# Cross attention: softmax sums from pairs of key tiles, experts moved by four to five steps, small products ahead of value and sum products in a step

## The chip, the cores and the metric

One Trainium2 chip, one of its cores. The metric is the device time of one execution of the whole program in microseconds, taken as the median of several runs.

## The reference

A decoder of two layers with a layer norm after each of six sublayers, on 8 batches of 256 tokens of width 512. The change touches the last but one sublayer, cross attention with the context, whose heads and positions are read crosswise (the 256 tokens are the channels, 512 features the positions), and the order of the last one, experts chosen by a router, beside it:

```python
qh = q.reshape(B, h, dq, Lq)          # B = 8 batches, h = 8 heads, dq = 32, Lq = 512
kh = k.reshape(B, h, dq, Lk)          # k = v = the context, Lk = 512
scale = 1.0 / jnp.sqrt(jnp.asarray(dq, dtype=q.dtype))
qk = jnp.einsum('bhdq,bhdl->bhql', qh, kh) * scale
sm = jax.nn.softmax(qk, axis=-1)
ret = jnp.einsum('bhql,bhdl->bhdq', sm, vh)
return gamma * ret
...
x = _layernorm(x + _L1_xattn_ref(x, ctx_2048, ctx_2048, L1_xattn_gamma), axis=-1)
x = _layernorm(x + _L1_ffn_ref(x, ...), axis=-1)   # top 2 of 8 experts of rank 16
```

## The kernel before, in words

All sublayers run one after the other in one program. The function of the change, `l1_cross_and_experts` (line 1799), does the last two together. Each engine has a queue of its own, written out by hand: all five walk the same list `steps()` (line 1882), 16 steps `g` per batch `b`, and at each step an engine does what its `if` lines name. Engines meet only at semaphores, so an engine's queue order is fixed and a wait in it holds all behind it.

A batch is two halves `t` of four heads (32 rows each, 128 partitions). A half has four key tiles `k` of 128 keys; a tile is four units (one per head), done in two steps of two units each. In a step TensorE makes, 11 steps ahead (`LEAD`), rough scores of two heads for 128 queries (`rough_scores`, L2358), from rounded operands; VectorE takes their maxima (`maxima`, L2212), which TensorE turns (`turn_largest`, L2366), ScalarE rounds (`round_largest`, L2129), and SyncE puts as a 97th row behind the stacked operands (`place_largest`, L1975). This is why the scores are made twice: the second time (`scores`, L2376) they come out transposed, keys on the partitions, with the maximum subtracted. The 96 other rows are high and low parts of x and context, copied together by `stack` (L1956): 24 copies of 128 KB per batch from SyncE's queue, for which `take_lo` (L1937, on GpSimd for batches 1 to 7) makes the low parts.

ScalarE takes the exponential of each unit (`exps`, L2135) into one of 12 buffers `pT`. Once per key tile TensorE multiplies four units with the values (`values`, L2388, into `v_ps`) and four units with a matrix of ones (L2391, into `d_ps`), which adds up the softmax's denominators over all four tiles. At the end of a half ScalarE reads both out (`read_out`, L2142 and L2145). The denominators take a detour: SyncE lays one row per head over partitions (`lay_sums`, L1985), VectorE inverts them (`invert`, L2221), SyncE writes them to memory (`keep_inverses`, L1991) and reads them back spread over the partitions (`spread_inverses`, L1999). GpSimd multiplies and adds the residual (`residual`, L2055 and L2061). The last half is inverted directly (L2218).

Then follow, for the batch before, the norm (`statistics` L2226, `power` L2067 to L2073, `apply` L2151) and the experts: `turn_x` (L2401), `turned` (L2157), `project` (L2412), `shift`, `exponential`, `gate`, `choose`, `picks`, `weigh` on VectorE and ScalarE, `turn_hidden` (L2420), `hidden` (L2171), `out` (L2429, L2430), `add_experts` (L2295), a second norm and `store` (L1966). Two banks `a_ps` serve rough scores and all of these products in turn, in the order of the steps (`slot_uses`); a product waits until the use before last of the banks has been read. The score products have two banks `s_ps`, one per unit: a unit waits for the exponential two units before.

## Time and profile before

| what | us |
|---|---|
| median of 3 runs | 2101.18 (2098.77 to 2101.21) |
| the profiled execution's own time | 2102.42 |
| its span, first to last instruction | 2100.3 |
| TensorE (PE) busy | 1864.2 (89%) |
| VectorE (DVE) busy | 1145.9 (55%) |
| ScalarE (ACT) busy | 851.1 (41%) |
| GpSimd (POOL) busy | 331.6 (16%) |

Busy time is the union of an engine's instructions over all sublayers. The granted clock is the share of TensorE's full clock of 2.4 GHz; at 0.5 it runs at 1.2 GHz. In the rows, L and a number is a line of the kernel, `out<-in` are the tiles it writes and reads, "x8" the records merged into one line, and in brackets stands how long the engine was idle before and which instruction or transfer ended that. SPq is the queue of transfers that SyncE issues; one product of two float32 operands is two records, so four products of values are "x8". TensorE's durations overlap each other, so its pace is read from start to start.

### The profile page before, as it was taken

The page shows a single profiled execution, that of the slowest core. Times are in us where ns is not written, and L with a number is a line of the kernel's source. Part 1 is how long each engine was busy: PE and PEld are TensorE (multiplying, and loading weights), DVE is VectorE, ACT ScalarE, POOL GpSimd, SP SyncE. Part 2 cuts the span into 40 slices and gives each one's busy share as a digit, 9 for nine tenths or more (in the row PEclk, how much of TensorE's full clock was granted, in tenths as well). Part 3 has the DMA queues.
Part 4 walks back from the last instruction along what each step waited for, and adds up shares of the span by engine and source line. Part 5 has one row for each costly group of instructions (what it writes and reads, how often), then busy time and mean ns, then how long its engine had stood idle before and what let it go on. Part 6 is the DMA issues. An engine that isn't in the chain of part 4 may idle for free. (4 is left out here: it accounts for less than half of the span.)

```text
span 2100.3 us, 30928 instructions
## 1 busy us (share of the span) xinstructions
PE 1864.2 (89%) x11568; PEld 1425.5 (68%) x11568; DVE 1145.9 (55%) x2133; ACT 851.1 (41%) x2040; POOL 331.6 (16%) x414
## 2 busy tenths in 40 slices
PE   6979999999976799999999987899996498899994
PEld 5869998998964688888888876677774133333332
DVE  3446444444435565555555436788876535555543
ACT  2225333333323343333333214666674145555552
POOL 0000000000011112111111001333332212223211
PEclk9989999999988899999999998999998589999997
DMA  3122000000012221111110013000101644444400
GB/s 103 44 97 71 21 21 21 21 21 21 26 54 78 83 79 46 36 31 41 46 36 16 11 41 120 11 32 32 51 21 61 174 115 102 112 115 124 102 22 25
DMA packets 83664, 119.83 MB, mean 57 GB/s; under 512 B 15221, under 2 KB 31221, under 8 KB 83517
## 3 DMA queue, kind: packets, MB, share of 16 engines
q1 hardware_dynamic: 83516, 117.86, 19.5%
q8 instruction: 93, 1.52, 0.3%
q14 instruction: 55, 0.44, 0.1%
HBM read 75.42 MB, written 16.98 MB: 44 GB/s over the span
## 5 line engine op out<-in xcount | busy, mean ns | idle before, releaser
L2212 DVE TENSOR_REDUCE e_nbx<-e_a_ps 128x2 f32<-128x1024 f32 x128 | 153.2, 1214 | 103.0 <-PE e_a_ps L2358 102.9
L1164 PE MATMUL yp<-ccy,toep 128*128 128x288 f32 x640 | 181.8, 435 | 19.7 <-POOL ccy L892 13.6
L2135 ACT ACTIVATE e_pT<-e_s_ps 128x512 f32<-128x512 f32 x256 | 139.0, 597 | 126.7 <-PE e_s_ps L2376 123.8
L1442 ACT ACTIVATE p<-p,nb,rq 128x128 f32<-128x128 f32 (+1 forms) x256 | 136.9, 541 | 94.8 <-DVE nb L1539 94.8
L1164 PEld LDWEIGHTS yp<-ccy,toep 128*128 128x128 f32 x640 | 126.0, 205 | 55.7 <-POOL ccy L892 14.8
L80 PE MATMUL q_ps<-a_xt_hi,wq_hi 128*128 128x256 f32 x512 | 151.7, 296 | 4.2 <-DVE wo_lo L112 4.1
L82 PE MATMUL q_ps<-a_xt_hi,wq_lo 128*128 128x256 f32 x512 | 146.5, 286 | 0.0
L81 PE MATMUL q_ps<-a_xt_lo,wq_hi 128*128 128x256 f32 x512 | 146.3, 286 | 0.0
L1062 DVE SCALAR_TENSOR_TENSOR hm<-gu_ps,us_col,sg 128x256 f32<-128x256 f32 x88 | 42.3, 480 | 184.1 <-ACT sg L971 184.1
L514 ACT ACTIVATE ex<-ex 128x512 f32<-128x512 f32 x64 | 40.4, 632 | 213.8 <-DVE ex L567 213.8
L1399 POOL TENSOR_TENSOR p<-p,rs 128x512 f32<-128x512 f32 x64 | 94.2, 1472 | 195.5 <-DVE rs L1546 195.5
L2376 PE MATMUL e_s_ps<-qs,ks 97*128 97x512 f32 x256 | 108.5, 485 | 18.4 <-DMA qs<-e_xh 14.2
L971 ACT ACTIVATE sg<-gu_ps,gs_col 128x256 f32<-128x256 f32 x88 | 41.6, 473 | 189.8 <-PE gu_ps L82 189.7
L545 DVE TENSOR_TENSOR tl<-t_ps,th 128x512 fp32r<-128x512 f32 x64 | 44.3, 692 | 132.7 <-ACT th L506 132.7
L80 PE MATMUL o_ps<-wo_hi,th 128*128 128x512 f32 x256 | 106.7, 417 | 1.9 <-DVE tl L545 1.9
L80 PE MATMUL gu_ps<-m_xt_hi,wg_hi 128*128 128x256 f32 x352 | 100.3, 285 | 8.2 <-DVE m_xt_lo L1054 8.2
L231 POOL TENSOR_TENSOR n_rstd<-n_mv,eps 128x2 f32<-128x2 f32 x16 | 3.1, 197 | 634.2 <-DVE n_mv L225 634.2
L80 PEld LDWEIGHTS q_ps<-a_xt_hi,wq_hi 128*128 128x128 f32 x512 | 99.9, 195 | 4.7 <-issue 4.5
L81 PE MATMUL o_ps<-wo_lo,th 128*128 128x512 f32 x256 | 101.2, 395 | 0.0
L82 PE MATMUL o_ps<-wo_hi,tl 128*128 128x512 f32 x256 | 101.1, 395 | 0.0
L80 PE MATMUL gu_ps<-m_xt_hi,wu_hi 128*128 128x256 f32 x352 | 100.1, 284 | 0.0
L81 PEld LDWEIGHTS q_ps<-a_xt_lo,wq_hi 128*128 128x128 f32 x512 | 99.8, 195 | 0.0
(296 smaller groups left out, 4904.7 us busy)
## 6 DMA issues: line engine op xcount, KB each, us to landing
x_after<-n_r SPq DMA_DIRECT2D x16, 512.0 KB, 2.8
toep<-padded_kernels SPq DMA_DIRECT2D x32, 256.0 KB, 3.6
qs<-e_xh SPq DMA_DIRECT2D x64, 128.0 KB, 2.5
ks<-e_ch SPq DMA_DIRECT2D x64, 128.0 KB, 2.5
x<-in_x SPq DMA_DIRECT2D x8, 512.0 KB, 4.3
a_x<-in_x SPq DMA_DIRECT2D x8, 512.0 KB, 4.5
ring<-in_wqT SPq DMA_DIRECT2D x8, 512.0 KB, 4.6
ring<-in_woT SPq DMA_DIRECT2D x8, 512.0 KB, 3.8
```

The source lines that it names most:

```text
L80: pe.matmul(out, whi, xhi, start=start, stop=False)
L81: pe.matmul(out, whi, xlo, start=False, stop=False)
L82: return pe.matmul(out, wlo, xhi, start=False, stop=stop)
L545: dve.tensor_tensor(tl[:], t_ps[:], th[:], ALU.subtract).then_inc(tl_done, 1)
L971: act.activation(sg[:], gu_ps[n % 2][:, 0, :], ACT.Silu, scale=gs_col[:, j:j + 1]).then_inc(sg_done, 1)
L1062: dve.scalar_tensor_tensor(hm[:], gu_ps[n % 2][:, 1, :], us_col[:, j:j + 1], sg[:], ALU.mult, ALU.mult).then_inc(hm_done, 1)
L1164: last = pe.matmul(yp[:, lo % 2, 0:NCOL], toep[h % 2][:, (lo - li) * P:(lo - li + 1) * P], ccy[h % 2][:, li, 0:NCOL], start=(li == 0), sto ...
L1399: pool.tensor_tensor(tile, tile, r, ALU.mult).then_inc(pn_done, 1)
L1442: act.activation(p[n % 3][:, h, part[t]], p[n % 3][:, h, part[t]], ACT.Exp, bias=nb[i][:, t, h:h + 1], scale=rq[u][:, t:t + 1], accum_out= ...
L2135: act.activation(pT[u % NPT][:], s_ps[u % 2][:], ACT.Exp).then_inc(e_done, 1)
L2212: dve.tensor_reduce(heads, slot("pair", n)[:], AX.X, ALU.max, negate=True).then_inc(nb_done, 1)
L2376: pe.matmul(s_ps[u % 2][:], ks[b % 2][0:KX, t, j, k * P:(k + 1) * P], qs[b % 2][0:KX, t, j, :], start=True, stop=True).then_inc(s_mm, 1)
```

## The change

Sums: instead of adding up four key tiles by four blocks of products with ones, GpSimd adds the exponentials of tiles 0 and 1 (`add_early`), VectorE those of tiles 2 and 3 (`add_late`), and TensorE makes two blocks of products per half (`sum_up`). The buffers of exponentials are 13 instead of 12; `nbr`, `dsb`, `vsb` and `rec` have one buffer instead of two. `scores` makes two units after one wait for both exponentials of the pair before. The values come one step later, and in a step they and the sums stand behind the small products. The experts of a batch, both norms, `read_out`, the inverses and `residual` come one to five steps later, and the list is five steps longer. At the start `stack(0)` stands ahead of `load(1)` and gamma, the weights come after `place_largest(0)`, and the two memsets of the operands' row of ones come later.

The diff, cut to its core (waits on renamed semaphores and the one-buffer indices are left out in part):

```diff
-NPT = 12
+NPT = 13
...
-        nbr = [sb(f"e_nbr{i}", [P, D], F32R) for i in range(2)]
+        nbr = sb("e_nbr", [P, D], F32R)
...
-        dsb = [sb(f"e_dsb{i}", [P, D]) for i in range(2)]
-        vsb = [sb(f"e_vsb{i}", [P, D]) for i in range(2)]
+        early = [sb(f"e_early{j}", [P, D]) for j in range(HT)]
+        late = [sb(f"e_late{j}", [P, D]) for j in range(HT)]
+        dsb, vsb = sb("e_dsb", [P, D]), sb("e_vsb", [P, D])
...
-        rec = [sb(f"e_rec{i}", [P, D]) for i in range(2)]
+        rec = sb("e_rec", [P, D])
...
+    stack(0)
     load(1)
     sp.dma_start(gcol[:], gamma.partition_broadcast(P)).then_inc(g_loaded, 16)
-    stack(0)
-    next_load(2)
-    residual(0)
...
     for b, step, g in steps():
+        if g == -1:
+            next_load(2)
+            residual(0)
...
         if step == 0 and 0 < b + 1 < B:
             stack(b + 1)
-        if step in (2, 10) and 0 <= 2 * b - 1 + step // 8 < LAST:
+        if step in (4, 12) and 0 <= 2 * b - 1 + step // 8 < LAST:
             lay_sums(2 * b - 1 + step // 8)
-        if step in (4, 12) and 0 <= 2 * b - 1 + step // 8 < LAST:
-            keep_inverses(2 * b - 1 + step // 8)
-        if step in (5, 13) and 0 <= 2 * b - 1 + step // 8 < LAST:
-            spread_inverses(2 * b - 1 + step // 8)
         if step in (6, 14) and 0 <= 2 * b + 1 + step // 8 < 2 * B:
             place_largest(2 * b + 1 + step // 8)
-        if step == 6 and 0 <= b - 2 < B:
+        if step in (6, 14) and 0 <= 2 * b - 1 + step // 8 < LAST:
+            keep_inverses(2 * b - 1 + step // 8)
+        if step in (7, 15) and 0 <= 2 * b - 1 + step // 8 < LAST:
+            spread_inverses(2 * b - 1 + step // 8)
+        if step == 9 and 0 < b + 1 < B:
+            residual(b + 1)
+        if step == 10 and 0 <= b and b + 3 < B:
+            next_load(b + 3)
+        if step == 11 and 0 <= b - 2 < B:
             store(b - 2)
-        if step == 8 and 0 < b + 1 < B:
-            residual(b + 1)
-        if step == 8 and 0 <= b and b + 3 < B:
-            next_load(b + 3)
     sp.wait_ge(stored, 16 * B)
...
+    def add_early(n, j):
+        u = UNITS // 2 * n + j
+        pool.wait_ge(e_done, u + HT + 1)
+        if n:
+            pool.wait_ge(d_mm, 2 * n - 1)
+        pool.tensor_tensor(early[j][:], pT[u % NPT][:], pT[(u + HT) % NPT][:], ALU.add).then_inc(early_done, 1)
...
-        if step == 4 and 0 <= b - 2 < B:
-            power(b - 2, mv6, mv6_done, y6_done, rstd6, ve6_done, rstd6_done, nm6, nm6_done)
-        if step == 6 and 0 <= b - 1 < B:
+        if step in (4, 5, 12, 13) and 0 <= b < B:
+            add_early(2 * b + step // 8, step % 2 * 2)
+            add_early(2 * b + step // 8, step % 2 * 2 + 1)
+        if step == 0 and 0 <= b - 1 < B:
+            residual(b - 1, 0)
+        if step == 8 and 0 <= b - 1 < B:
             residual(b - 1, 1)
         if step == 6 and b + 2 < B:
             scale_x(b + 2)
-        if step == 8 and 0 <= b - 1 < B:
+        if step == 9 and 0 <= b - 2 < B:
+            power(b - 2, mv6, mv6_done, y6_done, rstd6, ve6_done, rstd6_done, nm6, nm6_done)
+        if step == 10 and 0 <= b - 1 < B:
             power(b - 1, mv5, mv5_done, y5_done, rstd5, ve5_done, rstd5_done, nm5, nm5_done)
         if step == 10 and b + 2 < B:
             take_lo(pool, b + 2, "cl")
-        if step == 12 and b + 2 < B:
+        if step == 14 and b + 2 < B:
             take_lo(pool, b + 2, "xl")
-        if step == 14 and 0 <= b < B:
-            residual(b, 0)
...
     def exps(u):
         act.wait_ge(s_mm, u + 1)
         if u >= NPT:
+            n, k = divmod((u - NPT) // HT, NQ)
             act.wait_ge(pv_mm, (u - NPT) // HT + 1)
+            if k < 2:
+                act.wait_ge(early_done, HT * n + (u - NPT) % HT + 1)
+            else:
+                act.wait_ge(late_done, HT * n + (u - NPT) % HT + 1)
         act.activation(pT[u % NPT][:], s_ps[u % 2][:], ACT.Exp).then_inc(e_done, 1)
     def read_out(n):
         act.wait_ge(pv_mm, NQ * (n + 1))
-        if n >= 2:
-            act.wait_ge(laid[n % 2], 16 * HT * (n // 2))
-        act.activation(dsb[n % 2][:], d_ps[:], ACT.Copy).then_inc(o_read, 1)
-        if n >= 2:
-            act.wait_ge(added5, n - 1)
-        act.activation(vsb[n % 2][:], v_ps[:], ACT.Copy, scale=gcol[:]).then_inc(o_read, 1)
+        if n:
+            act.wait_ge(added5, n)
+        act.activation(vsb[:], v_ps[:], ACT.Copy, scale=gcol[:]).then_inc(v_read, 1)
+        act.wait_ge(d_mm, 2 * n + 2)
+        if n:
+            act.wait_ge(laid[(n - 1) % 2], 16 * HT * ((n - 1) // 2 + 1))
+        act.activation(dsb[:], d_ps[:], ACT.Copy).then_inc(d_read, 1)
...
     act.wait_ge(g_loaded, 16)
     for b, step, g in steps():
-        if step == 1 and 0 <= b - 2 < B:
+        if step == 5 and 0 <= b - 2 < B:
             hidden(b - 2)
-        if step == 11 and 0 <= b - 1 < B:
+        if step == 15 and 0 <= b - 1 < B:
             turned(b - 1)
         if 0 <= g < PAIRS_IN_ALL:
             exps(2 * g)
             exps(2 * g + 1)
-        if step in (2, 10) and 0 <= 2 * b - 1 + step // 8 < 2 * B:
+        if step == 1 and 0 <= b - 2 < B:
+            exponential(b - 2)
+        if step in (3, 11) and 0 <= 2 * b - 1 + step // 8 < 2 * B:
             read_out(2 * b - 1 + step // 8)
-        if step == 5 and 0 <= b - 2 < B:
-            apply(b - 2, nm6, nm6_done, rstd6, y6_done)
         if step in (5, 13) and 0 <= 2 * b + 1 + step // 8 < 2 * B:
             round_largest(2 * b + 1 + step // 8)
-        if step == 7 and 0 < b + 1 < B:
+        if step == 9 and 0 < b + 1 < B:
             context(b + 1)
         if step == 8 and b + 2 < B:
             round_hi(b + 2, "ch")
-        if step == 9 and 0 <= b - 1 < B:
+        if step == 10 and 0 <= b - 2 < B:
+            apply(b - 2, nm6, nm6_done, rstd6, y6_done)
+        if step == 12 and b + 2 < B:
+            round_hi(b + 2, "xh")
+        if step == 12 and 0 <= b - 1 < B:
             apply(b - 1, nm5, nm5_done, rstd5, y5_done)
-        if step == 10 and b + 2 < B:
-            round_hi(b + 2, "xh")
-        if step == 13 and 0 <= b - 1 < B:
-            exponential(b - 1)
 @block.vector
...
+    def add_late(n, j):
+        u = UNITS // 2 * n + 2 * HT + j
+        dve.wait_ge(e_done, u + HT + 1)
+        if n:
+            dve.wait_ge(d_mm, 2 * n)
+        dve.tensor_tensor(late[j][:], pT[u % NPT][:], pT[(u + HT) % NPT][:], ALU.add).then_inc(late_done, 1)
...
         dve.tensor_tensor(rr[b % 2][:], slot("out", b)[:], rr[b % 2][:], ALU.add).then_inc(added6, 1)
-    for u in range(2):
+    def one_row(u):
         dve.memset(ks[u][KX - 1:KX, :, :, :].bitcast(F32), 1.0).then_inc(set_up, 1)
     take_lo(dve, 0, "cl")
     take_lo(dve, 0, "xl")
-    dve.wait_ge(set_up, 5)
-    dve.wait_ge(g_loaded, 16)
+    dve.wait_ge(set_up, 3)
     for b, step, g in steps():
-        if step == 3 and 0 <= b - 2 < B:
+        if step == 1 and 0 <= b - 2 < B:
+            shift(b - 2)
+        if step == 8 and 0 <= b - 2 < B:
             add_experts(b - 2)
-        if step == 13 and 0 <= b - 1 < B:
-            shift(b - 1)
         if 0 <= g + LEAD < PAIRS_IN_ALL:
             maxima(g + LEAD)
+        if g == -3:
+            one_row(0)
         if b == 0 and step == 0:
+            one_row(1)
             dve.wait_ge(w_loaded, 64)
             dve.tensor_scalar(bias[:, 0, 0:E], bias[:, 0, 0:E], BONUS, None, ALU.add).then_inc(prepared, 1)
             dve.wait_ge(prepared, 3)
+        if step in (7, 15) and 0 <= b < B:
+            add_late(2 * b + step // 8, 0)
+            add_late(2 * b + step // 8, 1)
+        if step in (0, 8) and 0 <= 2 * b - 1 + step // 8 < 2 * B:
+            add_late(2 * b - 1 + step // 8, 2)
+            add_late(2 * b - 1 + step // 8, 3)
+        if step == 2 and 0 <= b - 2 < B:
+            gate(b - 2)
+            choose(b - 2)
         if step == 3 and 0 <= b - 2 < B:
+            picks(b - 2)
+            weigh(b - 2)
+        if step in (6, 14) and 0 <= 2 * b - 1 + step // 8 < 2 * B:
+            invert(2 * b - 1 + step // 8)
+        if step == 8 and 0 <= b - 2 < B:
             statistics(b - 2, added6, b - 1, st6, st6_done, mv6, mv6_done)
-        if step in (3, 11) and 0 <= 2 * b - 1 + step // 8 < 2 * B:
-            invert(2 * b - 1 + step // 8)
-        if step == 8 and 0 <= b - 1 < B:
+        if step == 10 and 0 <= b - 1 < B:
             statistics(b - 1, added5, T * b, st5, st5_done, mv5, mv5_done)
-        if step == 14 and 0 <= b - 1 < B:
-            gate(b - 1)
-            choose(b - 1)
-        if step == 15 and 0 <= b - 1 < B:
-            picks(b - 1)
-            weigh(b - 1)
...
-    def scores(u):
-        b, t, k, j = unit(u)
-        if k == 0:
-            pe.wait_ge(stacked[j], 16 * 6 * (b + 1))
-            pe.wait_ge(biased, 16 * HT * (T * b + t + 1))
-        if u >= 2:
-            pe.wait_ge(e_done, u - 1)
-        pe.matmul(s_ps[u % 2][:], ks[b % 2][0:KX, t, j, k * P:(k + 1) * P], qs[b % 2][0:KX, t, j, :],
-                  start=True, stop=True).then_inc(s_mm, 1)
+    def scores(g):
+        for u in (2 * g, 2 * g + 1):
+            b, t, k, j = unit(u)
+            if k == 0:
+                pe.wait_ge(stacked[j], 16 * 6 * (b + 1))
+                pe.wait_ge(biased, 16 * HT * (T * b + t + 1))
+        if g:
+            pe.wait_ge(e_done, 2 * g)
+        for u in (2 * g, 2 * g + 1):
+            b, t, k, j = unit(u)
+            pe.matmul(s_ps[u % 2][:], ks[b % 2][0:KX, t, j, k * P:(k + 1) * P], qs[b % 2][0:KX, t, j, :],
+                      start=True, stop=True).then_inc(s_mm, 1)
     def values(n):
...
         b, t, k, _ = unit(HT * n)
         pe.wait_ge(e_done, HT * (n + 1))
...
             pe.wait_ge(vt_done, b + 1)
         for j in range(HT):
             e = t * P + j * CX
-            pe.matmul(v_ps[j * CX:(j + 1) * CX, :], vt[b % 2][:, k, e:e + CX], pT[(HT * n + j) % NPT][:],
-                      start=(k == 0), stop=(k == NQ - 1), skip_group_check=True, tile_position=(0, j * CX))
+            last = pe.matmul(v_ps[j * CX:(j + 1) * CX, :], vt[b % 2][:, k, e:e + CX],
+                             pT[(HT * n + j) % NPT][:], start=(k == 0), stop=(k == NQ - 1),
+                             skip_group_check=True, tile_position=(0, j * CX))
+        last.then_inc(pv_mm, 1)
+    def sum_up(n, parts, done, first):
+        pe.wait_ge(done, HT * (n + 1))
+        if first and n:
+            pe.wait_ge(d_read, n)
         for j in range(HT):
-            last = pe.matmul(d_ps[j * CX:(j + 1) * CX, :], ones[:], pT[(HT * n + j) % NPT][:],
-                             start=(k == 0), stop=(k == NQ - 1), skip_group_check=True,
-                             tile_position=(0, j * CX))
-        last.then_inc(pv_mm, 1)
+            last = pe.matmul(d_ps[j * CX:(j + 1) * CX, :], ones[:], parts[j][:], start=first, stop=not first,
+                             skip_group_check=True, tile_position=(0, j * CX))
+        last.then_inc(d_mm, 1)
     def turn_x(b):
         pe.wait_ge(y5_done, T * b + T)
         if 0 <= g + LEAD < PAIRS_IN_ALL:
             rough_scores(g + LEAD)
         if 0 <= g < PAIRS_IN_ALL:
-            scores(2 * g)
-            scores(2 * g + 1)
+            scores(g)
         if g == 1:
             pe.wait_ge(set_up, 5)
-        if g % 2 and 0 <= (g - 3) // 2 < T * NQ * B:
-            values((g - 3) // 2)
         if step == 0 and 0 <= b - 2 < B:
+            project(b - 2)
+        if step == 4 and 0 <= b - 2 < B:
             turn_hidden(b - 2)
-        if step == 2 and 0 <= b - 2 < B:
-            out(b - 2)
         if step in (5, 13) and 0 <= 2 * b + 1 + step // 8 < 2 * B:
             turn_largest(2 * b + 1 + step // 8)
-        if step == 7 and 0 < b + 1 < B:
+        if step == 7 and 0 <= b - 2 < B:
+            out(b - 2)
+        if step == 9 and 0 < b + 1 < B:
             turn_context(b + 1)
-        if step == 10 and 0 <= b - 1 < B:
+        if step == 14 and 0 <= b - 1 < B:
             turn_x(b - 1)
-        if step == 12 and 0 <= b - 1 < B:
-            project(b - 1)
+        if g % 2 == 0 and 0 <= (g - 4) // 2 < T * NQ * B:
+            values((g - 4) // 2)
+        if step in (0, 8) and 0 <= 2 * b - 1 + step // 8 < 2 * B:
+            sum_up(2 * b - 1 + step // 8, early, early_done, True)
+        if step in (2, 10) and 0 <= 2 * b - 1 + step // 8 < 2 * B:
+            sum_up(2 * b - 1 + step // 8, late, late_done, False)
```

## Rows read from the trace of the kernel before

**Rows 1.** Stretches: length, busy PE, PEld, DVE, ACT, POOL, clock, DMA share, GB/s

```profile
1716.00:2052.00 336.00, 306.47 (x1658) 123.54 (x1658) 173.85 (x320) 187.00 (x333) 81.90 (x94) 0.94 0.39 100
1961.00:2009.00 48.00, 45.27 (x252) 18.21 (x254) 27.37 (x53) 26.59 (x49) 7.89 (x13) 0.96 0.41 101
```

**Rows 2.** Timeline, two steps of the loop in batch 1 (start, duration, both us)

```profile
1716.26 0.50 PE L2358 MATMUL e_a_ps<-e_ch,e_xh 32*128 32x512 f32 x2
...
1716.69 0.73 PE L2376 MATMUL e_s_ps<-qs,ks 97*128 97x512 f32 x2
...
1717.23 1.09 ACT L2135 ACTIVATE e_pT<-e_s_ps 128x512 f32<-128x512 f32 x2 [2.10 <-PE e_s_ps L2376]
...
1718.86 1.07 PE L2388 MATMUL e_v_ps<-e_pT,e_vt 128*32 128x512 f32 x8
...
1719.74 1.04 PE L2391 MATMUL e_d_ps<-e_pT,e_ones 128*32 128x512 f32 x8
...
1720.71 0.50 PE L2358 MATMUL e_a_ps<-e_ch,e_xh 32*128 32x512 f32 x2
```

**Rows 3.** Timeline, the turn of a batch on SyncE, VectorE and GpSimd

```profile
1715.17 0.67 SPq L1956 DMA_DIRECT2D qs<-e_xh  x1
...
1731.10 2.78 SPq L1985 DMA_DIRECT2D e_rcol<-e_dsb  x4
1735.07 0.25 DVE L2221 RECIPROCAL e_rcol<-e_rcol 128x16 f32<-128x16 f32 x1 [11.46 <-DMA e_rcol<-e_dsb]
...
1741.78 1.28 POOL L2055 TENSOR_TENSOR e_vsb<-e_vsb,e_rec 128x512 f32<-128x512 f32 x1 [25.95 <-DMA e_rec<-cross_sums]
```

**Rows 4.** Timeline of TensorE: a stall; project of batch 0 and of batch 6

```profile
1736.54 1.09 PE L2366 MATMUL e_a_ps<-ident,e_nbx 128*128 128x128 f32 x4 [4.66 <-DVE e_nbx L2212]
...
1757.29 2.02 PE L2412 MATMUL e_a_ps<-wrd,f_xT 128*128 128x136 f32 x16
...
2044.92 2.02 PE L2412 MATMUL e_a_ps<-wrd,f_xT 128*128 128x136 f32 x16
```

**Rows 5.** Groups of instructions by line in the last stage

```profile
L2391 PE MATMUL e_d_ps<-e_pT,e_ones 128*32 128x512 f32 x512 | 74.1, 652 | 0.0
...
L2055 POOL TENSOR_TENSOR e_vsb<-e_vsb,e_rec 128x512 f32<-128x512 f32 x16 | 20.5, 1279 | 148.0 <-DMA e_rec<-cross_sums 146.0 <-DVE e_rec L2218 2.0
...
L1937 POOL TENSOR_TENSOR e_cl<-e_c,e_ch 128x1024 fp32r<-128x1024 f32 x4 | 9.5, 2363 | 22.1 <-DMA ks<-e_cl 22.1
...
L1937 DVE TENSOR_TENSOR e_cl<-ring,e_ch 128x1024 fp32r<-128x1024 f32 x1 | 1.2, 1224 | 0.0
```

**Rows 6.** Timeline, statistics and power chain of batch 1

```profile
1798.04 1.28 DVE L2226 BATCH_NORM_STATS2 e_st<-e_r 128x6 f32<-128x512 f32 x2
...
1799.68 0.20 POOL L2067 TENSOR_TENSOR e_rstd<-e_mv,eps 128x2 f32<-128x2 f32 x1 [2.73 <-DVE e_mv L2229]
...
1800.76 0.20 POOL L2073 TENSOR_TENSOR e_nm<-e_nm,e_rstd 128x2 f32<-128x2 f32 x1
```

**Rows 7.** Timeline, the start of the last stage

```profile
1638.33 3.47 DVE L2298 MEMSET ks<- 1x4096 f32 x1 [0.80 <-DMA e_gamma<-in_gamma]
...
1644.22 0.70 SPq L1956 DMA_DIRECT2D qs<-e_xh  x1
...
1671.57 1.19 PE L2376 MATMUL e_s_ps<-qs,ks 97*128 97x512 f32 x2 [14.23 <-DMA qs<-e_xh]
```

**Rows 8.** Timeline, the end: last score products, turn_x of batch 7

```profile
2050.37 0.99 PE L2376 MATMUL e_s_ps<-qs,ks 97*128 97x512 f32 x2 [0.45 <-ACT e_pT L2135]
...
2072.69 1.97 PE L2401 MATMUL e_a_ps<-ident,e_r 128*128 128x128 f32 x8 [13.41 <-ACT e_r L2151]
```

**Rows 9.** Two stretches (columns as in rows 1), a record after the first

```profile
1867.70:1871.10 3.40, 1.74 (x9) 0.82 (x9) 2.62 (x11) 1.74 (x4) 0.23 (x1) 1.00 0.93 201
2027.00:2051.00 24.00, 20.52 (x130) 8.90 (x130) 5.34 (x26) 16.81 (x32) 4.54 (x8) 1.00 0.13 46
...
1871.94 1.94 PE L2388 MATMUL e_v_ps<-e_pT,e_vt 128*32 128x512 f32 x8
```

65 lines of the change are left out of this document (33 added, 32 removed).

## The prediction

> **What bounds the kernel now.** I read the stretches first. The change touches the last stage alone: the score products of its eight batches, from the first one at 1671.57 to the last at 2050.37, and the small products that ride along. In the steady part of it TensorE is busy 306.47 of 336 us, ScalarE 187.00, VectorE 173.85, GpSimd 81.90 [rows 1]; one batch (1961 to 2009) holds 45.27 us of TensorE work in 48. So TensorE's own list of work is the first bound, and what it waits for the second.
>
> Next the order of time on TensorE. Two steps of the loop (one key tile of 128 keys, four heads) run from 1716.26 to 1720.71, 4.45 us [rows 2]. By the starts: rough scores 0.43 (twice), score products 0.66 for the first pair, the second pair to 1718.86, values 0.88, sums 0.97. ScalarE's two exponentials begin 0.54 us after the first score product and take 1.09, so both are done 1.63 us after that start, and the following score product can begin at about 1.67.
>
> Then the waits. At the turn of a batch the SyncE queue issues 24 copies of `stack`, from 1715.17 to 1731.10, then the four of `lay_sums`; only then can VectorE's reciprocal run (1735.07), which stands in its queue at step 3, ahead of the maxima; GpSimd's product with the inverses follows at 1741.78 [rows 3]. TensorE stands 4.66 us for it at 1736.54 [rows 4]. From the `project` of batch 0 to that of batch 6, 1757.29 to 2044.92, six batches take 287.6 us: 47.9 each [rows 4]. Against 45.3 of work, 2.6 are waits.
>
> **The change, part by part**, against the profiled run's 2102.4 us (span 2100.3; the median of the runs shown is 1.2 lower).
>
> *Sums.* 64 blocks of sum products (512 records, 74.1 us) become 32 [rows 2, 5]: 32 x 0.97 = 31.0 us off TensorE, four blocks off each batch.
>
> *Score products in pairs.* Both now wait for both exponentials of the pair before. In an even step 0.88 of values and 0.43 of rough scores follow the first pair, and the wait is covered: 0.66 + 0.88 + 0.43 is more than 1.67. In an odd step only 0.66 + 0.43 = 1.09 stands before the next pair, so TensorE waits 0.58. Two steps without sums: 3.06 of work and 0.58 of wait, 3.64; with a sum block about 4.6. A batch then has 8 x 3.64 + 4 x 0.97 = 33.0 us for the loop. The other products are what is left of 45.27 after 8 x 4.45: 9.7 us. They now stand ahead of values and sums; four of them (two turns of maxima, `out`, `context`) fall in odd steps and fill the wait, 4 x 0.58 = 2.3 less. TensorE alone would need 40.4 us for a batch. The wait is bounded by zero and 0.58 per odd step; I keep 0.58, since it follows from rows.
>
> *Experts four to five steps later.* `project`, `turn_hidden`, `out` and the VectorE, ScalarE and GpSimd work between them keep their amount. What they buy is order: `project` and `out` now lie in steps 0 and 7, so TensorE has some 23 us of work (8 steps, of which two hold sums, plus `project`, `turn_hidden`, one turn and `out`) before it needs the maxima that stand behind the reciprocal, now at step 6. That is about the 20.2 us from the first copy to the reciprocal plus a maximum of 1.2 [rows 3]. The 4.66 us stall goes; what is late next is below.
>
> *New adds.* GpSimd gets 8 adds per batch at 1.28 (as its other 128x512 ones), 10.2 us. VectorE gets 8 of 128x512; the nearest row with two SBUF inputs is 1.22 for 128x1024, so between 0.6 and 0.7 each, 5.2 us [rows 5]. VectorE's busy time becomes 27.4 + 5.2 = 32.6 per batch: covered on average. GpSimd's are not covered, because its queue closes a ring: first copy of `stack` to the residual's first op 26.6 us [rows 3]; two ops of 1.28, 2.6; VectorE's statistics 1.6 and GpSimd's power chain 1.3 [rows 6]; `take_lo` of the context 2.4; four adds 5.2; `take_lo` of x 2.4, for which the next `stack` waits. Sum 42.1 us per batch, and before the change the same ring without the adds was about 37 and hidden. `vsb` has one buffer now, so ScalarE's read-out at step 11 waits for that residual too, 29.2 us after the first copy; TensorE reaches step 11 at about 31, so this costs nothing until the ring slips by 2 us.
>
> So a batch with `stack`, loads and experts is set by 40.4 (TensorE) and 42.1 (ring), which share waits; I add 2 us for steps with several long ScalarE operations (`round_hi` and `apply` both in step 12) and for engines that meet in the wrong order: 44.2 for batches 1 to 5. Batch 6 has no loads (42), batch 7 no `stack` either (41). Sum 304 against 335 now (1716.26 to 2051.3): 31 off.
>
> *The lock.* No row shows a GpSimd operation and a VectorE operation with two SBUF inputs at the same time. Between no cost and eight waits for a whole GpSimd add (10.2 us a batch, most inside VectorE's idle 15) I take 1, inside the 2 above. The Trainium skill, "SBUF — State Buffer", SBUF: two separate sides, says that a VectorE operation with two SBUF inputs and a GpSimd operation lock each other out for a whole instruction; no row here shows it, and by it each late add could lose up to one GpSimd operation.
>
> *Start.* VectorE's two memsets of one row (3.47 each) leave the way of the first `take_lo`, and `stack(0)` stands ahead of `load(1)` and gamma: its first copy, now 1644.22, can go at about 1637.7 [rows 7]. `place_largest(0)` passes the weights' loads, but waits for ScalarE, which waits for gamma and the later `load(1)`: about 1664 at best. First score product at 1668.5, not 1671.6: 3 off. Batch 0 has 2.7 us less on TensorE and a later `place_largest(1)`, behind weights and `stack(1)`: 2 off.
>
> *End.* From the last score product (end 2051.3) to `turn_x(7)` (2072.69) it is 21.4 us [rows 8]. Afterwards batch 6 still has `project`, the gates and `out` there, but the last reciprocal passes ahead of `add_experts(6)` and is done at about 10 us; `out(6)` ends near 11.6, its statistics 14.5, then power, apply and the same for batch 7: 19. 2.5 off; the rest of the chain stays.
>
> Sum: 5 + 31 + 2.5 = 38.5 off; 2063.9, by the median about 2063.
>
> **Rivals.**
> *TensorE alone sets it.* The ring is slack after all (the copies start as early as the scores allow, adds run early). Seven batches at 41: 287, 48 off, plus 8: about 2046. For it: the ring's longest part, 15.9 us of issue, already lay partly beside work before. Against: eight adds at 1.28 stand in it.
> *The ring slips.* Lock and late ScalarE work make it 46.5: seven batches 325, with the rest 2084. For it: GpSimd idles on the same transfer at 1741.78 that now gates ScalarE's read-out.
> *The clock: slower.* A stretch with TensorE busy 1.74 us (1867.70 to 1871.10) came before records at 1.2 GHz: 1871.94 took 1.94 us for values [rows 9], against 1.07 before. The change puts a wait of 0.58 into every second step. A batch has 40.4 us of work at 2.4 GHz; if a share f of the time is at 1.2 GHz, it takes 40.4/(1 - f/2). The granted clock of 0.96 now [rows 1] is f = 0.08. From f = 0.31 on a batch is over 47.9 and the kernel slower; at one half it is 54: 7 x 54 = 377, 42 more, 2137. Against: from 2027 to 2051 TensorE was busy 20.52 of 24 us, with waits on exponentials, and had 2.4 GHz throughout [rows 9]; the new pair of steps is 84% busy. The Trainium skill, "TensorE: Matmul & The Clock Gate", A second HAM failure mode, says that short idles between groups of matmuls, as with a cycled PSUM queue, can make the clock fall and rise again; the stretch from 2027 speaks against it here, the one from 1867.70 for it.
> *The change does nothing*: TensorE's removed blocks are refilled by waits to the last microsecond: 2101. The rows give no reason for such a balance.
>
> **How the numbers follow.** Forecast case 0.50, TensorE alone 0.20, ring slips 0.18, clock 0.08, nothing 0.02, other losses 0.02. Range 2038 (TensorE alone, and the half-clock stretches gone as well) to 2092 (ring slips, start and end give nothing). Faster by over 0.2% (4 us, about what a measurement can tell): 0.90. Within: 0.02. Slower: 0.08.
>
> **What would show it.** Sum products 256 records; 32 blocks. Two steps without sums take 3.6 us, with the score products waiting 0.5 to 0.6 for exponentials in odd steps. No 4 us stall behind the reciprocal. From `project` to `project` 44 us in the middle batches, with `take_lo` of x ending shortly before the next first copy. Late adds 0.65 us; if some take 2, the lock is real. The granted clock stays above 0.9 in the batches; if it is near 0.7, the third rival holds. If a batch takes 41, the first does. First score product near 1668.

## The result and the profile after

The changed kernel takes 2129.38 us (median of 4, 2121.72 to 2133.98) against 2100.43 (4 runs, 2098.77 to 2101.21) for the kernel before: ratio 1.0135, 95% interval 1.0100 to 1.0171. It is **slower** by 29 us. The forecast was 2063.0, the range ended at 2092, and "slower" had 8%. The profiled execution has a span of 2131.2 us. "Before" and "after" are these two kernels below; a line of before has a number up to 50 higher in after.

Where the start and the batches went, TensorE's timeline of after:

```profile
1666.95 1.19 PE L2417 MATMUL e_s_ps<-qs,ks 97*128 97x512 f32 x2 [2.93 <-DMA qs<-e_nbr]
...
1677.48 0.79 PE L2395 MATMUL e_a_ps<-e_ch,e_xh 32*128 32x512 f32 x2 [4.68 <-DVE e_nbx L2232]
...
1762.49 2.02 PE L2460 MATMUL e_a_ps<-wrd,f_xT 128*128 128x136 f32 x16
...
2080.91 2.02 PE L2460 MATMUL e_a_ps<-wrd,f_xT 128*128 128x136 f32 x16
...
2102.68 1.97 PE L2449 MATMUL e_a_ps<-ident,e_r 128*128 128x128 f32 x8 [7.26 <-ACT e_r L2171]
```

The first score product is 4.6 us earlier than in [rows 7]. From the `project` of batch 0 to that of batch 6 it is 318.4 us, 53.1 a batch, against 47.9 in [rows 4]. From the last `project` to `turn_x(7)` there are 21.8 us. (The `project` of a batch stands four steps later in after, so the start and the end can't be compared from it one by one.) These six batches took 30.8 us more, and the whole span grew by 30.9: the loss is in the batches.

The stretches (columns as in rows 1), and TensorE's waits from the second batch on (line waiting, who ended it: us in total, times, longest):

```profile
1716.00:2052.00 336.00, 278.65 (x1293) 119.81 (x1293) 218.01 (x335) 168.01 (x298) 143.82 (x137) 0.81 0.39 97
...
1760.00:1780.00 20.00, 13.01 (x76) 6.26 (x74) 18.08 (x31) 7.57 (x15) 9.32 (x7) 0.91 0.76 166
1780.00:1790.00 10.00, 10.00 (x34) 3.83 (x33) 3.48 (x5) 3.43 (x7) 0.00 (x0) 0.50 0.08 13
```

```profile
PE e_a_ps L2468 <- DVE f_hw L2316: 26.9, 6, 5.9
PE e_s_ps L2417 <- ACT e_pT L2154: 23.9, 32, 3.6
PE e_a_ps L2395 <- DVE e_nbx L2232: 8.2, 12, 1.3
PE e_s_ps L2417 <- DMA qs<-e_nbr: 3.8, 3, 2.0
```

The second wait is the forecast's: mostly 0.5 to 0.6 us for a pair's exponentials, in some four steps of a batch, those odd ones that no small product fills. The copies (`e_nbr`) hardly hold TensorE: the ring is not what makes a batch 53 us long. The first is new: `turn_hidden` waits for the gated values, 26.9 us in six batches, where the kernel before waits 5.6 us. TensorE stands there in order, with score products behind it. And the granted clock over the batches is 0.81, where [rows 1] show 0.94.

Why are the gated values late? The groups of the gates on VectorE, with those of the adds and sums (line, operation, count | busy us, mean ns | idle before):

```profile
L2072 POOL TENSOR_TENSOR e_early<-e_pT 128x512 f32<-128x512 f32 x64 | 79.6, 1274 | 21.3 <-ACT e_pT L2154 21.3
...
L2240 DVE TENSOR_TENSOR e_late<-e_pT 128x512 f32<-128x512 f32 x64 | 42.1, 699 | 6.7 <-ACT e_pT L2154 6.7
...
L2440 PE MATMUL e_d_ps<-e_early,e_ones 128*32 128x512 f32 x128 | 18.4, 651 | 0.0
L2440 PE MATMUL e_d_ps<-e_late,e_ones 128*32 128x512 f32 x128 | 18.0, 638 | 0.0
...
L2313 DVE TENSOR_TENSOR f_w<-f_pick 128x16 f32<-128x16 f32 x8 | 7.9, 987 | 0.3
L2298 DVE TENSOR_TENSOR f_pick<-f_numbers,f_chosen 128x32 f32<-128x32 f32 x8 | 7.7, 960 | 0.0
...
L2302 DVE TENSOR_TENSOR f_share<-f_top,f_tsum 128x4 f32<-128x4 f32 x8 | 5.7, 711 | 0.0
...
L2308 DVE TENSOR_TENSOR f_pick<-f_pick,f_share 128x32 f32<-128x32 f32 x8 | 5.3, 665 | 0.9
```

Adds and sums are as predicted: 1274 and 699 ns, and 36.4 us of sum products instead of 74.1 [rows 5]. But four tiny operations that the change moves but doesn't alter, 4 to 32 elements per partition, take 0.67 to 0.99 us on average. In the kernel before:

```profile
L2262 DVE TENSOR_TENSOR f_tsum<-f_top 128x2 f32<-128x2 f32 x8 | 4.4, 550 | 0.0
...
L2270 DVE TENSOR_TENSOR f_pick<-f_numbers,f_chosen 128x32 f32<-128x32 f32 x8 | 1.5, 192 | 0.0
L2280 DVE TENSOR_TENSOR f_pick<-f_pick,f_share 128x32 f32<-128x32 f32 x8 | 1.5, 192 | 0.9
...
L2285 DVE TENSOR_TENSOR f_w<-f_pick 128x16 f32<-128x16 f32 x8 | 1.4, 175 | 0.3
...
L2274 DVE TENSOR_TENSOR f_share<-f_top,f_tsum 128x4 f32<-128x4 f32 x8 | 1.2, 155 | 0.0
```

One passage of after, in order of time on all engines:

```profile
1771.68 1.21 DVE L2232 TENSOR_REDUCE e_nbx<-e_a_ps 128x2 f32<-128x1024 f32 x1
1771.70 4.95 POOL L2072 TENSOR_TENSOR e_early<-e_pT 128x512 f32<-128x512 f32 x4
...
1772.91 0.15 DVE L2296 RECIPROCAL f_tsum<-f_tsum 128x2 f32<-128x2 f32 x1
...
1773.03 1.22 DVE L2298 TENSOR_TENSOR f_pick<-f_numbers,f_chosen 128x32 f32<-128x32 f32 x1
...
1774.17 1.27 DVE L2302 TENSOR_TENSOR f_share<-f_top,f_tsum 128x4 f32<-128x4 f32 x1
...
1775.55 1.14 DVE L2308 TENSOR_TENSOR f_pick<-f_pick,f_share 128x32 f32<-128x32 f32 x1
...
1776.60 1.90 POOL L2048 TENSOR_TENSOR x<-x,e_scale 128x1024 f32<-128x1024 f32 x1
...
1776.73 1.80 DVE L2313 TENSOR_TENSOR f_w<-f_pick 128x16 f32<-128x16 f32 x1
...
1778.56 0.49 DVE L2316 SCALAR_TENSOR_TENSOR f_hw<-f_lh,f_w 128x128 f32<-128x128 f32 x2
...
1779.11 0.48 PE L2468 MATMUL e_a_ps<-ident,f_hw 128*128 128x128 f32 x1 [5.36 <-DVE f_hw L2316]
...
1780.16 1.93 PE L2429 MATMUL e_v_ps<-e_pT,e_vt 128*32 128x512 f32 x8
```

While GpSimd makes its four early adds, each VectorE operation with two SBUF inputs lasts until a GpSimd operation ends: 1.1 to 1.3 us beside an add, 1.80 beside the 1.90 us of `scale_x`. The reciprocal (one SBUF input) and the reduction from PSUM keep their durations. `f_hw` is some 4.7 us late (5.43 us in the four rows, 0.71 before), TensorE idles 5.36, and then it runs at 1.2 GHz from 1780 to 1790 (granted clock 0.50): a value block takes 1.93 us in place of 1.06. The Trainium skill, "SBUF — State Buffer", SBUF: two separate sides, describes just this: the port pair shared by VectorE and GpSimd is "an **exclusive lock**, not a bandwidth split", held for the whole instruction. These rows agree.

This passage is typical: four of the six waits for `f_hw` are 5.2 to 5.9 us. In the other two (1999.67, 2051.51) they are 2.5 us: there GpSimd paused for 0.4 us between the second and the third add, and only the cast of `f_chosen` (1.26 us) and the first `f_pick` (1.21) were held up. The cast has one SBUF input, so operations with two are not the only ones that pay.

### The profile page after: what moved, and what is told of

The parts are those of the page before. It is cut to its first block and busy times, and to the rows that moved or that the text cites. A ratio compares the mean times of both kernels' runs of the same rounds, so it can differ in the third digit from the quotient of the medians.

```text
span 2131.2 us, 30696 instructions
## 1 busy us (share of the span) xinstructions
PE 1864.4 (87%) x11312; PEld 1435.3 (67%) x11312; DVE 1211.8 (57%) x2197; ACT 850.3 (40%) x2040; POOL 410.5 (19%) x478
## 5 line engine op out<-in xcount | busy, mean ns | idle before, releaser
L2417 PE MATMUL e_s_ps<-qs,ks 97*128 97x512 f32 x256 | 111.0, 520 | 31.1 <-ACT e_pT L2154 23.9
L545 DVE TENSOR_TENSOR tl<-t_ps,th 128x512 fp32r<-128x512 f32 x64 | 44.2, 691 | 132.4 <-ACT th L506 132.4
L2395 PEld LDWEIGHTS e_a_ps<-e_ch,e_xh 32*128 32x128 f32 x256 | 27.9, 217 | 122.2 <-issue 76.3
L2395 PE MATMUL e_a_ps<-e_ch,e_xh 32*128 32x512 f32 x256 | 76.5, 600 | 31.3 <-DVE e_nbx L2232 15.6
L567 DVE TENSOR_SCALAR ex<-q_ps,bq_col 128x256 f32<-128x256 f32 x128 | 55.8, 477 | 81.2 <-PE q_ps L82 81.2
```

The lines of the kernel that those rows point to most:

```text
L567: dve.tensor_scalar(ex[p % 2][:, h, :], q_ps[p % 2][:, h, :], bq_col[:, head:head + 1], 0.0, ALU.add, ALU.min).then_inc(mq_done, 1)
L2395: last = pe.matmul(bank[:, i, :], xh[b % 2][d, t, q * P:(q + 1) * P], ch[b % 2][d, t, :], start=True, stop=True, skip_group_check=True, ti ...
L2417: pe.matmul(s_ps[u % 2][:], ks[b % 2][0:KX, t, j, k * P:(k + 1) * P], qs[b % 2][0:KX, t, j, :], start=True, stop=True).then_inc(s_mm, 1)
```

## The experiments

Theory L (lock): the early adds make the gates late, TensorE waits in order, and the clock falls behind it. Theory P: the paired score waits cost more than they should. Theory A: it is the added work itself. Theory O: the experts' new order leaves too little time between the gates and their turn. "Half-clock time" is the time at 1.2 GHz from 30 us after the first score product to the last one: 41.0 us before, 134.4 after. It comes from the one profiled execution of each kernel, and executions of one kernel differ in it: the profiled one of run 12, its slowest, has 92 us, though the kernel is the fastest by its median. Ratios are against the kernel before, run beside each kernel on the same chip; there it took 2099.7 to 2103.0 us, so kernels of different runs are compared by their ratios.

**1. All adds on VectorE.**

```diff
-    # gpsimd, steps 4, 5, 12, 13: add_early(...)   (in words)
+    # vector, steps 4, 5, 12, 13: add_early(...)   (in words)
```

> The changed kernel with all 64 early adds on VectorE (its steps 4, 5, 12, 13) instead of GpSimd. Theory L (a GpSimd add locks out each VectorE operation with two SBUF inputs; the gate's small operations take 1 us instead of 0.2, TensorE stands 4 to 6 us a batch for the turned gates and then falls to 1.2 GHz): the small operations return to 0.15 to 0.2 us, the wait of the turn of the hidden layer falls from 33 us in all to below 10, the slow-clock time in the batches from about 130 to below 60 us, the time from 2129 to about 2075. Theory P (the wait for both exponentials lowers the clock): the small operations return too, but the slow stretches stay, about 2120. Theory O (the new order of the experts, one step between the gates and their turn): the wait stays above 20 us, about 2120.

Measured: 2094.75 us, ratio 0.9983 (0.9956 to 1.0010). The waits for `f_hw` fall to 3.7 us in the batches, half-clock time to 71.9. The gates' four operations are back at 155 to 325 ns on average, although VectorE now makes the early adds as well (64 at 893 ns, 57 us). Taking the adds off GpSimd wins 32 to 35 us, by ratio and by median. The direction is theory L's, its size is not (2075, and under 60 us at half clock); theory O is out, since the wait for `f_hw` goes although the order stays.

**2. Each score product waits for its own exponential**, as before the change.

```diff
-    if g: pe.wait_ge(e_done, 2 * g)    # once for the pair
+    scores(2 * g); scores(2 * g + 1)   # each with its own wait
```

> The changed kernel, but each score product waits only for the exponential two units before, as in the kernel before. Theory P: the slow-clock stretches shrink and the time falls by 20 us or more. Theories L and O: the wait of the gates' turn stays at 33 us and the slow stretches after it too; the time changes by less than 10 us, at 2120 to 2129.

Measured: 2125.11 us, ratio 1.0125 (1.0087 to 1.0163). Waits for exponentials fall from 23.9 us in 32 to 8.4 in 8, waits for `f_hw` stay at 30.5 us in 6. The medians differ by 4 us from after, less than the two intervals, so the paired waits don't explain the 29 us. Half-clock time is about 109 us in the profile, 25 less than after, but the mean clock over all executions is 0.923 against 0.921.

**3. No adds**, the four sum blocks of a half as before; all other moves kept.

```diff
-    sum_up(n, early, ...); sum_up(n, late, ...)
+    # in values(n): four products of ones with pT
```

> The changed kernel with the sums as before: four blocks of products with ones per half, no adds on GpSimd or VectorE; all other moves stay. 31 us of TensorE work come back at full clock. Theory L: without adds nothing locks, the gates' turn waits below 10 us in all, so despite the work the time is at or below that of the kernel before, 2085 to 2100. Theory P: the paired scores are still there, but sums fill every second step; about 2110. Theory O: the wait stays above 20 us, 2140 or more.

Measured: 2095.40 us, ratio 0.9982 (0.9967 to 0.9997). Waits for `f_hw` 8.7 us in 6, half-clock time 54.6. Score products still wait 21.4 us in 33 for the exponentials of pairs. So neither the moves of work nor the paired waits make the kernel slower without the adds.

**4. Each GpSimd add cut into four** of 128 columns; same engine, same data.

```diff
-    pool.tensor_tensor(early[j][:], ...)                # 128x512
+    for c in range(4): pool.tensor_tensor(early[j][:, 128 * c:128 * (c + 1)], ...)
+    # the fourth waits for the three before it
```

> The changed kernel with each early add on GpSimd cut into four of 128 columns. Theory L, if the lock is held for one instruction: a small VectorE operation waits for at most about 0.4 us instead of 1.27, so their longest falls from 1.2 to 1.8 us to below 0.8 and the gates' turn waits some 15 us less; 2100 to 2115, though GpSimd's own adds cost more by their fixed parts. If contention is shared by time and not by instruction, the small operations stay as long as they are and the time at 2129 or above. Theories P and O: no effect on the wait, 2129 or above.

Measured: 2106.19 us, ratio 1.0023 (1.0000 to 1.0046), half-clock time 82.9, waits for `f_hw` 10.0 us in 6 (the profiled execution took 2095.1).

```profile
L2075 POOL TENSOR_TENSOR e_early<-e_pT 128x128 f32<-128x128 f32 x192 | 82.6, 459 | 17.5 <-ACT e_pT L2161 17.4
...
L2078 POOL TENSOR_TENSOR e_early<-e_pT 128x128 f32<-128x128 f32 x64 | 29.7, 464 | 5.0
...
L2305 DVE TENSOR_TENSOR f_pick<-f_numbers,f_chosen 128x32 f32<-128x32 f32 x8 | 3.0, 371 | 0.0
...
L2320 DVE TENSOR_TENSOR f_w<-f_pick 128x16 f32<-128x16 f32 x8 | 2.5, 315 | 0.3
```

GpSimd is busy 33 us more, and yet the kernel is 23 us faster than after. The tiny operations follow the length of one GpSimd instruction (960 to 371 ns), not GpSimd's load. None of the four took more than 0.48 us. That is against theory A, against theory O, and against a port that is shared by time; it is what "for the whole instruction" means.

**5. All adds on VectorE and unit score waits.**

```diff
+    # edits 1 and 2 together
```

> The changed kernel with all adds on VectorE (as in the first experiment, which gave 0.9983) and, beside that, each score product waiting for its own exponential again, as before the change. Theory L (the lock explains the loss; what is left beside it is the waits of the pairs): with both gone TensorE's waits of score products for exponentials fall from 22.6 us in 34 to under 9, as in the second experiment (8.4 in 8), and the batches get 10 to 14 us shorter than with paired waits: 2080 to 2085, ratio about 0.992, half-clock time well under the 72 us of the first experiment. Rival A (ScalarE and VectorE order the batches, not TensorE's waits on pairs): the waits move to other instructions, the time stays at 2092 to 2097.

Measured: 2093.18 us, ratio 0.9955 (0.9931 to 0.9979). The waits for exponentials do fall, to 4.8 us in 4, but 2080 to 2085 doesn't come. The rival of this run holds: part of the wait moves elsewhere. Of the 17.8 us that the exponentials give back (22.6 to 4.8), 6.4 come back as waits for `f_hw` (3.7 to 10.1) and 0.9 as waits for maxima (12.5 to 13.4); the rest isn't accounted for.

**6. One wait more.** The early adds of a first half begin behind the gated values:

```diff
     def add_early(n, j):
...
+        if n % 2 == 0 and n >= 4:
+            pool.wait_ge(hw_done, n - 2)
         pool.tensor_tensor(early[j][:], ...)
```

> The changed kernel with one wait added and nothing else: from batch 2 on, GpSimd's four early adds of a batch's first half start only when VectorE has made the gated hidden values of the batch that is in the experts. Same adds, same engines, same work, but the four adds no longer stand beside the small VectorE operations. Theory L: the small operations are back at 155 to 325 ns, TensorE's wait for the gated values falls from 33 us in 8 to under 10, half-clock time from 134 us to about 85, and the kernel is at 2095 to 2105 (ratio 0.998 to 1.002) although GpSimd does its adds later than before. Rival A (it is the amount of new work on GpSimd and VectorE that costs): no gain, or a loss since exponentials wait longer for the adds: 2130 or more.

Measured: **2088.34 us, ratio 0.9936 (0.9909 to 0.9963)**, 41 us below after, with the same work on each engine. Half-clock time 79.2. Timeline, groups and waits of this kernel:

```profile
1819.89 0.19 DVE L2300 TENSOR_TENSOR f_pick<-f_numbers,f_chosen 128x32 f32<-128x32 f32 x1
...
1820.00 0.15 DVE L2304 TENSOR_TENSOR f_share<-f_top,f_tsum 128x4 f32<-128x4 f32 x1
...
1820.27 0.19 DVE L2310 TENSOR_TENSOR f_pick<-f_pick,f_share 128x32 f32<-128x32 f32 x1
1820.49 0.18 DVE L2315 TENSOR_TENSOR f_w<-f_pick 128x16 f32<-128x16 f32 x1
...
1821.37 4.97 POOL L2074 TENSOR_TENSOR e_early<-e_pT 128x512 f32<-128x512 f32 x4 [9.08 <-DVE f_hw L2318]
```

```profile
L2074 POOL TENSOR_TENSOR e_early<-e_pT 128x512 f32<-128x512 f32 x64 | 79.6, 1273 | 47.9 <-DVE f_hw L2318 33.2 <-ACT e_pT L2156 14.7
```

```profile
PE e_s_ps L2419 <- ACT e_pT L2156: 25.3, 34, 3.5
PE e_a_ps L2397 <- DVE e_nbx L2234: 9.1, 16, 1.3
PE e_s_ps L2419 <- DMA qs<-e_nbr: 3.0, 3, 1.1
PE e_a_ps L2470 <- DVE f_hw L2318: 2.4, 6, 0.4
PE e_v_ps L2431 <- issue: 2.1, 1, 2.1
```

GpSimd now waits 33.2 us for the gates, and the score products wait no longer for it (25.3 us in 34, in after 23.9 in 32); `turn_hidden` waits 2.4 us in place of 26.9. (These waits are from the second batch to 2035.) Theory A is out: only the time of these adds, and of what follows them in GpSimd's queue, has changed.

**7. The lock by itself**: the kernel before, with four idle additions on GpSimd at the gates. Their result is read by nobody. Each waits for the one before (`spared`, left out here).

```diff
+    if step == 14 and 0 <= b - 1 < B:
+        pool.wait_ge(den_done, 2 * b)
+        for i in range(4): pool.tensor_tensor(spare[1][:], spare[0][:], spare[0][:], ALU.add)
```

> The kernel before the change, with four additions of 128x512 (one constant tile to itself, into a spare tile nobody reads) put on GpSimd in each batch, to start when VectorE begins the gates. Nothing waits for them but GpSimd's own next work, which is the product with the inverses some 15 us later. Theory L: the small VectorE operations with two inputs in SBUF take about 1.2 us each in place of 0.17 to 0.2, operations on one input stay, the gated values come 4 to 5 us later, TensorE waits for them (5.6 us in all before) 25 to 35 us in all, half-clock time rises from 41 us to 80 or more, and the kernel is slower by 15 to 35 us: 2115 to 2135. Rival A (GpSimd's adds cost through their own queue, not through a lock): VectorE's operations keep their durations and the time stays within 4 us of 2100.

Measured: 2113.20 us, ratio 1.0056 (1.0034 to 1.0078): 10 to 12 us slower, a miss in size.

```profile
1759.97 4.58 POOL L2111 TENSOR_TENSOR e_spare<-e_spare 128x512 f32<-128x512 f32 x4
1760.09 0.98 DVE L2280 TENSOR_TENSOR f_pick<-f_numbers,f_chosen 128x32 f32<-128x32 f32 x1
1760.99 0.15 DVE L2284 TENSOR_TENSOR f_share<-f_top,f_tsum 128x4 f32<-128x4 f32 x1
...
1761.26 0.93 DVE L2290 TENSOR_TENSOR f_pick<-f_pick,f_share 128x32 f32<-128x32 f32 x1
```

Here the adds wait for one another, and in the gap between two of them VectorE's next operation gets in (`f_share` 0.15). So about half the operations pay; TensorE waits 19.7 us in 6 for `f_hw` (5.6 before), half-clock time is 51.2. The rival is out: both `f_pick` operations take 0.93 to 0.98 us in place of 0.19. The mechanism needs none of the change's other parts, and its size depends on how the two engines' operations fall.

**8. As 5, with the router's weights loaded ahead of the loop**, since VectorE waits 5.2 us for the bias at the start of after.

```diff
-    if g == -1: ... four loads counted by w_loaded
+    # the four loads right behind gamma's
```

> As the first kernel of this call (all adds on VectorE, unit score waits), with the loads of the router and down weights and their biases issued before the loop instead of at its last step ahead of batch 0. In the changed kernel VectorE waits 5.2 us for the bias, in its queue ahead of the maxima, and TensorE 4.7 us behind it, at 1677. Theory L: that wait goes, first batch 3 to 5 us shorter, so 3 to 5 us below the first kernel of this call: 2076 to 2081. Rival A (the start is hidden again by what comes behind it, or the loads delay the copies ahead of the first score product): no more than 1 us of difference.

Measured: 2092.65 us, ratio 0.9954 (0.9926 to 0.9983), the same as run 5. Run 5 waited 4.05 us for the bias and TensorE 3.54 behind it; both waits are gone, but `project` of batch 0 starts only 0.85 us earlier (1756.63, in run 5 1757.48). What the start gains is hidden again by what follows.

**9. As 6, with unit score waits.**

```diff
+    # edits 6 and 2 together
```

> The changed kernel with the one wait of the sixth experiment (GpSimd's early adds of a first half behind the gated values; 2088.3, ratio 0.9936, half-clock time 79 us in the batches, TensorE waiting 25.3 us in 34 for exponentials), and each score product waiting for its own exponential again. Theory P (the waits of the pairs are part of what is missing to 2063, and they pull the clock down): waits for exponentials fall under 9 us, half-clock time under 65 us, 2078 to 2084. Theory S (what is missing comes from steps where ScalarE has several long operations, and from the clock after them; the short waits of the pairs are filled by nothing but cost little): 2085 to 2090, as with all adds on VectorE, where the same edit brought 2 us or less.

Measured: 2086.68 us, ratio 0.9924 (0.9895 to 0.9954). Waits for exponentials 9.8 us in 9, just above theory P's 9; half-clock time 60.8, as theory P had it; time as theory S had it.

**10. As 6, with the rounding of x two steps later on ScalarE.**

```diff
-    if step == 12 and b + 2 < B:
+    if step == 14 and b + 2 < B:
         round_hi(b + 2, "xh")
```

> The sixth experiment's kernel with one ScalarE operation moved: the rounding of x (1.08 us) from step 12, where it stands with the 1.54 us of the application of the normalisation, to step 14. In the sixth experiment's trace TensorE waits up to 3.5 us for exponentials around there and records at 1.2 GHz follow for 10 to 14 us in four of the batches. Theory S: the longest wait for exponentials falls to about 2.5 us, half-clock time from 79 to under 65 us, time 2078 to 2085. Theory P: no gain, 2086 to 2092, or a loss if GpSimd's take_lo of x, now behind the later rounding, holds up the next stack.

Measured: 2084.80 us, ratio 0.9925 (0.9896 to 0.9955). Longest wait for exponentials 3.2 us, not 2.5; half-clock time 58.0 and the time are as theory S had them, but the gain on run 6 is within the intervals, and the mean clock over all executions is the same (0.933, in run 6 0.932). The profiled execution (2077.3 us) shows something else: `take_lo` of x now waits for the later rounding, and the next first copy starts 0.3 us after it ends in five batches of five, where run 6 has 1.5 to 4.1 us between them. So here the copies do wait for this operation.

**11. As 6, with rough products made twice** (same result).

```diff
-    for i in range(2):
+    for i in (0, 1) if n % 2 else (0, 1, 0, 1):
```

> The sixth experiment's kernel with the two rough score products of every odd step made twice, with the same result: 0.43 us more of TensorE work in each step in which it waits 0.5 to 0.6 us for the exponentials of the pair, 3.4 us of extra work per batch. Theory C (short waits in every second step are what brings the clock down): waits for exponentials fall by half or more, half-clock time falls from 79 towards the 41 us of before, and the kernel is no slower than 2088 in spite of 28 us of added work, perhaps 2080. Rival (the clock falls after the single long waits of 1.3 to 3.5 us only, the short ones are harmless): half-clock time stays at 70 to 85 us and the time is 2088 to 2095.

Measured: 2092.34 us, ratio 0.9959 (0.9936 to 0.9982); waits no shorter, 27.6 us in 38. The doubled products had fallen into the step where values already cover the wait, so this run doesn't test shorter waits. TensorE has about 0.23 us more in every second step, 15 us in all, and the kernel is 4 us slower, within the intervals. Yet half-clock time is 44.8 us in the profile and the mean clock over all executions 0.937, in run 6 0.932: the clock rose although the waits stayed.

**12. As 6, with the edits of 9 and 10.**

```diff
+    # edits 6, 2 and 10 together
```

> The sixth experiment's kernel with both edits: unit score waits and the rounding of x in step 14. If P and S each hold, their gains add up: 2070 to 2080. If only one holds, the time is that of the better of the two kernels before it. If neither does, 2086 to 2092.

Measured: **2082.71 us, ratio 0.9902 (0.9873 to 0.9930)**, the lowest of all, 20 us below the kernel before beside it and some 47 below after. Its interval still overlaps that of run 6, and it doesn't decide whether both gains add up: that was to give 2070 to 2080, one of them alone 2084.8. Single executions lie between 2073.5 and 2095.7.

**13. As 11, in the other step**, where the waits are.

```diff
-    for i in range(2):
+    for i in (0, 1, 0, 1) if n % 2 else (0, 1):
```

> The sixth experiment's kernel with the two rough score products made twice in the other step of each two, directly ahead of the score products that wait 0.5 us for a pair's exponentials (the eleventh run had doubled them where nothing waits: 0.23 us more per step, waits unchanged at 27.6 us in 38, half-clock time 45 us in its profile, 2092.3). Theory C (the short waits keep the clock down): the waits halve at least, half-clock time is well under 79 us, 55 or less, and the time is under 2085. Rival (only the longer waits bring the clock down; the short ones are just lost time): waits for exponentials halve, half-clock time stays between 60 and 90 us, time 2086 to 2092, since the doubled products only stand where TensorE was idle.

Measured: 2085.90 us, ratio 0.9938 (0.9917 to 0.9959). A short wait is now 0.29 us in place of 0.51, their sum 20.4 us. Half-clock time in the profile is 55.1, and the mean clock of the whole program over all its runs is 0.937 (8 runs) against 0.932 in run 6 (6 runs) and 0.944 in the kernel before. So the clock rises, as theory C said, but it rose as much in run 11, whose waits stayed. That the short waits are what keeps it down is not shown: it was higher with repeated products in either step. And it brings no time: the ratio is that of run 6 (0.9936).

## Why the prediction was wrong

**The step that failed: "*The lock.*"** The forecast bounded it by eight waits for a whole GpSimd add, 10.2 us a batch, "most inside VectorE's idle 15", and took 1. Two things were wrong in it.

- *Who is locked out.* It put the price on the late adds. They took 699 ns on average, as predicted; the sign it offered, late adds of 2 us, hardly came (the longest of 64 took 1.76). Locked out were the gates, tiny operations in a chain, each paying up to one whole GpSimd instruction: 5.43 us for 0.71 of work in the passage shown.
- *Cover by average.* VectorE's idle time elsewhere in the batch doesn't help a chain on which `turn_hidden` waits in TensorE's order. "The experts keep their amount" was true of the work and not of its duration: their new place, steps 2 and 3, is just where the exponentials release the early adds. Here the change added a GpSimd burst and moved the gates into it at once.

"No row shows" the collision was wrong too: the row of `f_tsum` above, 550 ns for two elements beside a residual on GpSimd, shows it in the kernel before. It had been read past. One of its eight, beside the residual's product:

```profile
1765.11 1.29 POOL L2055 TENSOR_TENSOR e_vsb<-e_vsb,e_rec 128x512 f32<-128x512 f32 x1 [7.63 <-DMA e_rec<-cross_sums]
...
1765.84 0.58 DVE L2262 TENSOR_TENSOR f_tsum<-f_top 128x2 f32<-128x2 f32 x1
```

It ends at 1766.42, as the product on GpSimd does (1766.40).

**What the lock cost.** From `project` to `project` a batch takes 53.1 us in after and 46.7 in run 6: 6.4 us a batch where the forecast took 1. Run 6 takes 45.9 us off the profiled span (2131.2 to 2085.3). Waits for `f_hw` give 24.5 of it (26.9 to 2.4). Half-clock time falls by 55.2 us, worth at most 27.6 at half speed. Together 52 at most. The direct wait is measured; that the other 21 us came through the clock fits this sum and is not shown by itself.

**The rival of the clock** (2137) was nearest in time, by luck, and had the wrong cause. It had the clock fall from 0.58 us in every second step, from f = 0.31 on. After has a granted clock of 0.81 in its batches, f = 0.38, but run 2 takes those short waits away and is still at 2125, and run 6 keeps them and is at 2088. In the profiles f is 0.29 in run 2 and 0.23 in run 6, both below the bound, but over all executions only run 6 has a higher clock (0.932; run 2 0.923, after 0.921). So the greater part of the lost clock goes with the waits of 5 us; the short waits' part is not settled.

**The rest of the gap, 2088 to 2063.** With the lock avoided, `project` to `project` is 280.4 us for six batches in run 6 (1757.64 to 2038.03), 46.7 each; the forecast for these six is 4 x 44.2 + 42 + 41 = 259.8. The stretch of run 6:

```profile
1716.00:2035.00 319.00, 279.24 (x1384) 120.83 (x1383) 197.99 (x351) 181.63 (x325) 153.01 (x151) 0.88 0.41 104
```

TensorE is busy 279.24 of 319, 40.9 us per batch, and idle 5.8. The forecast's 44.2 was 38.1 of work (8 x 3.06, 4 x 0.97, 9.7) and 6.1 idle. The idle sum is right, partly by luck, since its parts are others: 3.5 for exponentials, 1.3 for maxima, 0.4 for copies, 0.3 for the gated values, where the ring of 42.1 was to bind. The ring's length was about right (from a first copy to the end of `take_lo` of x 43.2 to 46.1 us in run 6), but there the next copy starts 1.5 to 4.1 us later, so it isn't what holds a batch. It isn't far from it: in run 10, where the copies do wait for `take_lo` of x, the six batches take 270.7 us, 45.1 each, in an execution of 2077.3 us. The busy sum is 2.8 short, and the clock can account for it: 0.88 is 24% of the time at 1.2 GHz, the first stretch of [rows 1] shows 12%, and 12% of 46.7 more at half speed makes 2.8. (Against the second stretch, from which the forecast took its 45.27, it would be 3.7.) The forecast took its records from stretches at or near 2.4 GHz and priced no loss of clock from its own new waits. That is how the busy times add up; but in runs 11 and 13 a higher clock (0.937 in place of 0.932) brought no shorter time, with about 15 us of repeated work beside it. How much the clock and the waits each hold of these 20 us stays open.

**Point by point.** Sums halved: right, 36.4 us. Odd-step wait of 0.58: right, mostly 0.51 to 0.61. First copy 1637.7: 1638.6. Stall of 4.66 us behind the reciprocal: gone, right. Adds 1.28 and 0.6 to 0.7: right. First score product 1668.5: 1666.95, earlier, but the weights' later load costs a 4.68 us stall at 1677.48 that the forecast had only in part; run 8 says it matters little. Ring 42.1: 43 to 46 in run 6, not the bound there. A batch of 44.2: 53.1, and 46.7 without the lock.
